# A fused quantised layer, attention and experts kernel: the seam between attention and the shared expert becomes one block

## The reference, cut to what matters

```
x = x + experts0(layernorm(x), tokens, ctx)
x = x + quantised_ffn(layernorm(x))
x = x + attention(layernorm(x), ctx, Wq, Wg, bg, Wkv, Wo)     # out = (attn * sigmoid(gate)) @ Wo.T
h = layernorm(x)
scores = softmax(h @ gate_w.T); keep the 4 largest, normalise them
shared = (silu(h @ sw_gate) * (h @ sw_up)) @ sw_down          # inner width 704
routed = sum over the token's 4 experts: weight * ((silu(h @ w_gate) * (h @ w_up)) @ w_down)
x = x + shared + routed
```

## Time and profile before

| | us |
|---|---|
| median of 3 runs (lowest, highest) | 1134.96 (1133.03, 1137.04) |
| the profiled execution | 1136.04 |
| its span, first to last instruction | 1134.3 |
| PE busy | 1048.9 (92%) |
| DVE busy | 675.6 (60%) |
| ACT busy | 587.2 (52%) |
| POOL busy | 263.0 (23%) |

### The profile page before, as it was taken

One profiled execution on the slowest core, in us unless ns is written; L12 is line 12 of the kernel. 1 busy time (PEld: TensorE's weight loads), 2 busy tenths in 40 slices (PEclk: granted clock), 3 DMA queues, 4 the chain that ended last, 5 costly groups with the idle time before them and its releaser, 6 DMA issues. The chain is left out here.

```text
span 1134.3 us, 16229 instructions
## 1 busy us (share of the span) xinstructions
PE 1048.9 (92%) x5830; PEld 825.4 (73%) x5830; DVE 675.6 (60%) x1226; ACT 587.2 (52%) x886; POOL 263.0 (23%) x445
## 2 busy tenths in 40 slices
PE   7999899992999999989999977999989999999994
PEld 5888787771455555568888865788778899999993
DVE  6645455542899998665556555436842666666660
ACT  5655477781789888853333213311112466666651
POOL 1011122213555554100000004400010033333322
PEclk9999999996999999999999997999989999999998
DMA  6565166542000010201111113220132688888852
GB/s 218 190 231 171 41 174 195 160 147 94 19 29 19 20 29 10 95 1 66 47 65 52 73 56 95 96 75 29 47 113 77 217 225 229 227 226 227 228 131 38
DMA packets 47478, 127.03 MB, mean 112 GB/s; under 512 B 5810, under 2 KB 6834, under 8 KB 46644
## 3 DMA queue, kind: packets, MB, share of 16 engines
q1 hardware_dynamic: 36228, 96.99, 25.6%
q0 software_dynamic: 10608, 28.12, 11.3%
q10 hardware_dynamic: 576, 1.05, 0.3%
HBM read 97.76 MB, written 28.38 MB: 111 GB/s over the span
## 5 line engine op out<-in xcount | busy, mean ns | idle before, releaser
L1197 PE MATMUL bank<-w,f_qT 128*128 128x512 bf16 x512 | 119.2, 382 | 1.0 <-ACT f_qT L1013 0.7
L1197 PEld LDWEIGHTS bank<-w,f_qT 128*128 128x128 bf16 x512 | 49.0, 98 | 52.9 <-issue 2.6
L1754 POOL DMA_INDIRECT out<-e_y,scatter_idx x32 | 51.1, 1597 | 138.2 <-ACT e_y L1851 133.4
L1790 ACT ACTIVATE s_m_h<-s_mid 128x512 fp32r<-128x512 f32 (+1 forms) x24 | 15.1, 631 | 126.9 <-DVE s_mid L2104 76.2
L1742 POOL DMA_INDIRECT e_xg<-xn_rows,gather_idx x32 | 31.8, 995 | 172.4 <-DVE gather_idx L2094 104.7
L54 PE MATMUL bank<-wkv_h,ctx_h_all 128*128 128x512 f32 x128 | 52.3, 409 | 8.9 <-DVE wkv_l L705 7.4
L1216 PE MATMUL bank<-w,f_q2T 128*128 128x512 bf16 x256 | 57.9, 379 | 2.4 <-ACT f_q2T L1037 2.4
L54 PE MATMUL bank<-e_xT_h,e_wg_h 128*128 128x256 f32 (+1 forms) x192 | 56.4, 294 | 2.9 <-issue 2.0
L1385 DVE SCALAR_TENSOR_TENSOR f_h<-bank,f_columns,f_sg 128x512 f32<-128x512 f32 x64 | 47.9, 749 | 12.3 <-PE bank L1197 6.2
L55 PE MATMUL bank<-e_xT_l,e_wu_h 128*128 128x256 f32 (+1 forms) x192 | 54.0, 281 | 0.0
L54 PE MATMUL bank<-e_xT_h,e_wu_h 128*128 128x256 f32 (+1 forms) x192 | 54.0, 281 | 0.0
(11 more groups left out here) (394 smaller groups left out, 3295.1 us busy)
## 6 DMA issues: line engine op xcount, KB each, us to landing
wraw<-in_wffn SPq DMA_DIRECT2D x48, 512.0 KB, 4.0
e_raw_g<-in_ew_gate SPq DMA_DIRECT2D x16, 704.0 KB
e_raw_u<-in_ew_up SPq DMA_DIRECT2D x16, 704.0 KB
e_raw_d<-in_ew_down SPq DMA_DIRECT2D x16, 512.0 KB
sorted_y<-e_y SPq DMA_DIRECT2D x19, 256.0 KB
x_rows<-rows SPq DMA_DIRECT2D x16, 256.0 KB, 2.0
xn_rows<-a_work SPq DMA_DIRECT2D x16, 256.0 KB, 2.0
s_raw<-x_rows SPq DMA_DIRECT2D x16, 256.0 KB, 2.8
```

Of the source, the lines that this page charges most:

```text
L1197: ins = pe.matmul(bank[c % 2][:, :], qT[t % 2][:, k * P:(k + 1) * P], w_gv(k, col + c * 512), start=(k == 0), stop=(k == KD - 1))
L1754: gp.indirect_dma_start(io["out"], bass.IndirectOffsetOnAxis(g.scatter_idx[:, slot:slot + 1], 0), e_y[t][u][:, :], None, compute_op=ALU.ad ...
L1790: ins = act.activation(m[0][r, c, :], mid[n % 2][r, :], ACT.Copy)
```

## The change

The blocks of attention and of the shared and routed experts become one. The function of the experts no longer opens a block; it returns for each engine its pieces (`split_w`, `expand`, `activate`, `product_low`, ...) and a `body`, and the attention block calls them at the end of its own loops.

- SP loads pieces 0 to 9 in steps 11 to 15 of the attention loop, behind the writes of the step; the rest after it.
- ACT splits pieces 0 and 1 at the end of step 13, 2 and 3 in step 14, 4 and 5 in step 15; POOL makes their low halves between its small operations.
- The loop ends after step 15. PE's steps 16 to 18 are written out, with chunks 0, 1 and 2 of batch 0 between them. ACT and DVE have the matching orders. The scores (`shift`, `softmax`, `best`) come after chunk 2, `ties`, `masks`, `weights` and `orders` after products 3, 4, 5 and 6.
- The barrier and the clear between the blocks go. Instead, engines wait for single events before a place in SBUF gets new contents: all buffers of the experts are laid over attention's (the new cursors), the rows of tokens 0 to 1535 have their own semaphore (`EARLY`), and each weight buffer is filled when its attention weight is done with.

```diff
@@ sync
+                shared = stage["sync"](sp)
+                pieces_loaded = {n: () for n in range(TT)} | {11: (0, 1, 2), 12: (3, 4), 13: (5, 6), 14: (7, 8), 15: (9,)}
...
                     sp.wait_ge(x3_ready, s + 1)
-                    sp.dma_start(g.x3_dram[tokens(s), :], g.rows[:, s, :]).then_inc(x3_out, 16)
+                    sp.dma_start(g.x3_dram[tokens(s), :], g.rows[:, s, :]).then_inc(x3_out if s < EARLY else x3_late, 16)
                     sp.wait_ge(axn_ready, s + 1)
                     sp.dma_start(g.xn_dram[tokens(s), :], a_xn[s % 2][:, :]).then_inc(xn_out[s % 2], 16)
-                sp.wait_ge(x3_out, 16 * TT)
+                    if s == 11:
+                        sp.wait_ge(n_ready, EARLY)
+                    for n in pieces_loaded[s]:
+                        shared["load_piece"](n)
+                for n in range(10, shared_pieces):
+                    shared["load_piece"](n)
...
@@ gpsimd
                     gp.tensor_tensor(a_rstd[:, :], a_var[:, :], g.minus_half[:, 0:1], ALU.pow).then_inc(arstd_ready, 1)
+                    if EARLY <= s < TT - 1:
+                        shared["split_w"](2 * (s - EARLY))
+                        shared["split_w"](2 * (s - EARLY) + 1)
+                gp.wait_ge(x3_out, 16 * EARLY)
+                shared["clear"]()
+                for n in range(6, shared_pieces):
+                    shared["split_w"](n)
...
@@ scalar
                     if s >= 3:
                         logits(s - 3)
+                    if s > EARLY:
+                        if s == TT - 1:
+                            act.wait_ge(gate_ready, TT)
+                        shared["split_w"](2 * (s - EARLY) - 2)
+                        shared["split_w"](2 * (s - EARLY) - 1)
+                split_att(TT - 1)
+                act.wait_ge(x3_out, 16 * EARLY)
+                shared["activate"](0)
+                shared["split_w"](6)
+                shared["split_w"](7)
+                a_split_x(TT - 2)
+                logits(TT - 3)
+                shared["activate"](1)
+                act.wait_ge(ao_ready, TT)
+                shared["split_w"](8)
+                shared["split_w"](9)
+                a_split_x(TT - 1)
+                logits(TT - 2)
+                shared["activate"](2)
+                act.wait_ge(q_lo, TT)
+                shared["split_w"](10)
+                shared["split_w"](11)
+                logits(TT - 1)
+                shared["softmax"]()
+                shared["activate"](3)
+                shared["split_w"](12)
+                shared["split_w"](13)
+                shared["activate"](4)
+                shared["split_w"](14)
+                act.wait_ge(x3_late, 16 * (TT - EARLY))
+                shared["split_w"](15)
+                shared["activate"](5)
+                shared["split_w"](16)
...
@@ tensor
+                turn_att(TT - 1)
+                pe.wait_ge(nz_ready, 2 * TT)
+                pe.wait_ge(th_ready, TT)
+                pe.wait_ge(qf_ready, TT)
+                shared["expand"](0, 0)
+                project(TT - 1)
+                a_turn_x(TT - 2)
+                route(TT - 3)
+                shared["expand"](0, 1)
+                a_turn_x(TT - 1)
+                route(TT - 2)
+                shared["expand"](0, 2)
+                route(TT - 1)
+                shared["body"]()
...
@@ vector
+                split_att(TT - 1)
+                v.wait_ge(x3_out, 16 * EARLY)
+                shared["product_low"](0)
+                a_statistics(TT - 1)
+                a_normalise(TT - 1)
+                a_split_x(TT - 2)
+                shared["product_low"](1)
+                a_split_x(TT - 1)
+                shared["product_low"](2)
+                v.wait_ge(l_copied, TT)
+                for u in range(2):
+                    v.wait_ge(xn_out[u], 8 * TT)
+                shared["body"]()
...
@@ shared_experts1
-    PAIRS = E1 // 2
+    PAIRS, seam_chunks = E1 // 2, 3
...
@@ vector, shared(), the start of body()
             shift()
             softmax()
             best()
+            for n in range(seam_chunks, LAST):
+                product_low(n)
+                if n == seam_chunks:
+                    ties()
+                if n == seam_chunks + 1:
+                    masks()
+                if n == seam_chunks + 2:
+                    weights()
+                if n == seam_chunks + 3:
+                    orders()
```

More of the change, by code:

```diff
@@ L792, in ffn0_attention @@
         xn = low.some(2, "f0_xn", [P, D], fp32)
+        smalls = low.at
         stats, mv = low.some(3, "f0_stats", [P, 6], fp32), low.some(3, "f0_mv", [P, 2], fp32)
@@ L809, in ffn0_attention @@
         a_stats, a_mv = low.take("a1_stats", [P, 6], fp32), low.take("a1_mv", [P, 2], fp32)
+        raw_q_at = low.at
         after_wq = Cursor(nc, low.at)
@@ L831, in ffn0_attention @@
         a_q = [[x[:, part, :] for part in range(2)] for x in (q_first, q_second)]
+        places = {"rows": g.rows_at, "q_first": ffn_rows, "e": ffn_rows_end, "q_second": wide, "smalls": smalls, "raw_q": raw_q_at,
+                  "wq": g.w3_at, "wg": g.w3_at + 8 * KD * D, "wo": g.w3_at + 16 * KD * D}
+        stage = shared_experts1(nc, g, io, lambda name: sem(f"s_{name}"), places)
+        shared_pieces = stage["pieces"]
         norm_in = sem("norm_in")
@@ L1163, in _ @@
                 tanh(0)
-                for s in range(TT + 3):
-                    if 1 <= s <= TT:
+                for s in range(TT):
+                    if s:
                         split_att(s - 1)
@@ L1175, in _ @@
                         logits(s - 3)
+                    if s > EARLY:
[31 more added lines that the diff above has]
+                shared["split_w"](16)
+                for n in range(SFT, B * SFT):
+                    shared["activate"](n)
+                shared["body"]()
             @block.tensor
             def _(pe):
+                shared = stage["tensor"](pe)
                 def turn_q(t):
@@ L1327, in _ @@
                 gate(0)
-                for s in range(TT + 3):
-                    if 1 <= s <= TT:
+                for s in range(TT):
+                    if s:
                         turn_att(s - 1)
-                    if s < TT:
-                        attend(s)
+                    attend(s)
                     if s + KD < TT:
                         query(s + KD)
-                    if 1 <= s <= TT:
+                    if s:
                         project(s - 1)
@@ L1542, in _ @@
                 v.tensor_tensor(r_hl[:, :, E1:2 * E1], r_raw[:, :, :], f(r_hl[:, :, 0:E1]), ALU.subtract).then_inc(r_lo, 1)
-                for s in range(TT + 2):
-                    if 1 <= s <= TT:
+                for s in range(TT):
+                    if s:
                         split_att(s - 1)
-                    if s < TT:
-                        a_weigh(s)
+                    a_weigh(s)
                     if s + KD < TT:
@@ L2231, in program @@
         g.xT_l = keep(ctx, "xT_l", [P, KD, T], f32r)
-        with ExitStack() as rows:
-            g.rows = keep(rows, "rows", [P, TT, D], fp32)
-            ffn0_attention(nc, g, io)
-        shared_experts1(nc, g, io)
+        g.rows_at = (nc.sbuf_base + 63) // 64 * 64
+        g.rows = keep(ctx, "rows", [P, TT, D], fp32)
+        ffn0_to_experts1(nc, g, io)
 def laid_out(inputs):
```

1147 lines of the change are left out of this document (575 added, 572 removed).

## The result

The changed kernel takes 1124.77 us (median of 4 executions, 1119.68 to 1125.93); the kernel before took 1135.58 beside it (4 executions, 1133.03 to 1137.04). The ratio is 0.989, 95% interval 0.988 to 0.991: 10.8 us faster. Forecast were 1120.2 us and a range from 1115.5 to 1125.5. The time lies inside the range, 4.6 us above the forecast.

The account below looks back on a forecast made before the run. PE's idle and low clock at the seam between the blocks bound the kernel. Moving the contraction's start from 730.27 to 715.5 gains 14.8 us, including the loop's +1.6; 1134.96 less 14.8 gives 1120.2 us, range 1115.5 to 1125.5.

Parts of the forecast that it names:

- own range: Whole kernel: the narrower range of the main forecast, 1118 to 1122.5 us, given a chance of 0.67.
- rival B: Loop, scores and piece 16: POOL's low parts hold DVE longer; gain 10.7, 1124.3 us, at worst 1128.4; chance 0.16.
- The bound and the measure: Seam between the blocks: idle PE bounds it; batch 0's contraction start measures the change, moving from 730.27 to 715.5.
- Part 1: Attention loop, steps 13 and 14: ACT's splits delay the attention copy 0.8 each, +1.6 us in all; bounds 0 and 2.6.
- Part 2: Tail of attention: PE runs without idle through chunk 2, ending at 691.1 where before it ended at 707.99.
- Part 3, holds: Scores on DVE: POOL's low parts of pieces 10 and 11 hold a two-SBUF-tile operation, adding 0.85.
- Part 3, table switches: ACT's silu, exp, silu around the scores: added switches of 1.28 each cost nothing; bounds 0 and 2.6.
- no further term: End of the merged block: all semaphores cleared once, with no cost added beyond the barrier's removal.
- value nothing: New buffer addresses: -1 to +1 us over some hundred operations, counted as nothing; added table switches were valued likewise.
- A: Before the contraction: full cover, PE finds pieces 14 to 16 ready at 711.1; gain 20.8, 1114.2 us; chance 0.12.
- C: Attention loop: the three raw buffers make ACT wait for piece transfers; slower, say 1139 us; chance 0.05 with other losses.

Follow-up runs that it names:

- second sitting: The changed kernel run again unchanged, with a second trace, beside the kernel before; 1124.61 us, ratio 0.988 to the kernel before.
- down weights swapped: Against the changed kernel, only SBUF places change: down weights 0 and 1 behind the products' buffer, 2 to 5 in Wo's old place; 1124.57 us.
- third kernel: Against the changed kernel: ties, masks and weights one product later, piece 16 split before chunk 5's silu, count behind the contraction; 1118.46 us.
- second kernel: Against the changed kernel: in steps 13 to 15 ACT splits its two pieces right after the attention copy, not after the logits copy; 1121.76 us.
- quiet POOL: Against the changed kernel: POOL's low parts from piece 10 on wait until DVE has handed the scores to ACT's exp; 1126.81 us.

## Why the prediction was right, and where its size was off

**The number.** 1124.77 lies inside the range of 1115.5 to 1125.5, but near its upper end (two of the four executions lie beyond it, at 1125.88 and 1125.93), and outside the forecast's own range (1118 to 1122.5), next to what rival B would give (1124.3). B's mechanism isn't in the trace, and the upper end had been widened for B. So that the range held the loss behind the seam, which the prediction didn't have, is in part luck. Against the kernel before beside it, the gain was 10.8 us here, 13.2 in the second sitting and 12.1 with the down weights swapped, for a forecast of 14.8.

**The bound and the measure: right.** Measured from the last transposes, each step of the chain came within 0.3 us. (The terms as the prediction lists them add up to 715.3, not 715.5, which changes nothing here.) Forecast, then measured: product of chunk 2 at 22.8 and 23.05; product of chunk 3 at 32.05 and 32.18; product of chunk 5 at 43.8 and 43.99; contraction at 47.9 and 48.03. The idle before the contraction was 3.29 for a forecast of 3.4. The third kernel took the idle away by later routing steps and an earlier last split, which are both on that chain.

**Part 1: right in kind, 0.4 too large.** Two idles of 0.73 came for 0.8 each; 0.12 of each stood there before. The second kernel shows that the splits' place makes them.

**Part 2: right.** No idle to 707. The kernel without chunks between the passes prices them at 14.4 us, 6.93 idle and most of the rest clock.

**Part 3, holds: right in sum, not in place.** The forecast had one operation held by 0.85. Two were held, by 0.59 and 0.52, 0.26 more together, since POOL's two low parts begin apart (693.79 and 695.05). Rival B would have needed far more. Taking POOL away from the scores gained 0.66 in the seam. An operation with one operand in PSUM isn't held: the low half of the normalised row took 0.69 at 687.83, across the border of two low parts on POOL (686.87 and 688.11). The Trainium skill (SBUF — State Buffer, Who interferes with whom) says that an operation with at most one SBUF input, outside the two-port modes, does not contend with GpSimd, which is POOL here, and this trace agrees.

**Part 3, table switches: right.** The exp's load ends at 695.62, before its operand is ready; the silu's operation starts 0.01 after its load, and DVE's product follows at 700.97. The drain of 1.38 us that the Trainium skill names (ScalarE: Activation LUTs, What ACT_TABLE_LOAD costs) isn't to be seen: the load at 697.27 starts 0.02 after the exp ends.

**The step that failed: "no further term", and "value nothing" behind the seam.** The prediction took the seam's 14.8 us as the whole effect. The contraction's gain over the last transposes less the loop is 16.22 - 1.22 = 15.0, so that sum was right. Between the contraction and the end, however, 1.81 and 1.54 were lost. Of the 1.81, five more matmuls at the lower level (12 and 7, 0.19 each as in the prediction) are 1.0, and the wider spacing of the contraction's tiles is up to another 1.0; the second trace, with 7 such matmuls, lost 0.92. The prediction had valued both the slow matmuls and the new addresses at no change. The 1.54 stand at the end of the kernel, where the prediction named the single clear and gave it nothing. With the 1.55 of scatter ahead of the seam the account of this trace is 15.0 - 1.81 - 1.54 - 1.55 = 10.1. So 3.35 and 2.64 us of the shortfall lie behind the seam in the two traces of the changed kernel. The part at the end comes in every merged kernel. The part between goes with the slow matmuls: where the wait left none of them (quiet POOL, down weights swapped) that stretch took 390.27 and 390.25, less than the 391.95 of before with its 7. Why the tiles are wider, what decides the number of slow matmuls and how much of the end is the clear stays open.

**The rivals.** None of the three occurred. The prediction held ACT's order against A. With that order eased (piece 16 ahead of the silu) and the routing later, 1116.67 was reached, near A's 1114.2; which of the two edits does how much wasn't taken apart. C's waits of ACT for a piece's transfer show nowhere in the loop of the changed kernel. They do where ACT splits earlier (1.31 to 2.06 us), under waits that ACT has anyway.

## What to carry to other kernels

Follow the chain behind a seam to the first point where the order of work is the same again, and measure from there: steps read so from rows of before were right to 0.3 us. Then look for what stands outside that point, at the end of the kernel too; a resource that two blocks had apart is paid somewhere. Here, merging two blocks brought nothing by itself; what paid was independent work of the later one in the waits of the earlier, and small vector steps moved to where nobody waits for the engine.

## What the runs showed of the hardware that was not expected

- The same wait of PE, 3.27 to 3.29 us before the same contraction, left 0, 7, 12 or 13 matmuls at the lower clock level in different executions (0 with the down weights swapped and with the quiet POOL, 7 in the second trace of the changed kernel and without chunks between, 12 in the first, 13 with the splits in the wait). Only the changed kernel was traced twice, and it alone shows both 7 and 12. In kernels without the wait there were none. Such a wait costs its length and up to about 2.5 us more (13 x 0.19), and lets the time scatter.
- A scan of DVE beside POOL's low parts takes 3.68 us for 16 small operations; with POOL on for part of the time, as in the third kernel, 2.58; with POOL idle 1.46 (736.64 in the changed kernel). A tensor-scalar operation, whose input and output lie in SBUF, is held as well (710.23 in the changed kernel took 1.27; 0.29 in the third kernel, with POOL done; and the normalisation 1.49 for 0.55 above). So holds aren't only for two SBUF tiles, as the prediction read its rows.
- Idles of 6.93 us in attention's last passes cost about another 6.7 in clock: as much again as the idles themselves.
